# Two residual convolution layers on one core: block buffers made and first blocks loaded between the layers, a ring of three split eighths, another order of table loads, undivided stores

## The chip, the cores and the metric

The program runs on one core of one Trainium2 chip. Its metric is the device time of one execution in microseconds (us), over the whole program; less is better. TensorE (PE) multiplies matrices, VectorE (DVE) and ScalarE (ACT) work on elements, GpSimd (POOL) fills buffers and issues the stores here, and SyncE (SP) issues nearly all loads.

## The reference, cut to what matters

The input `x` is (8, 32, 512, 512) in float32. Each of two layers normalises in groups of two channels and adds its result to its input:

```python
# layer 0
x = x + quantised_conv3x3(group_norm(x))        # rounds to steps of S_X, S_OUT; clips to int8
# layer 1: g = group_norm(x)
feat = einsum('bihw,oi->bohw', g, conv_w) + conv_b        # pointwise, 32 -> 32 channels
filt = einsum('kh,bchw,lw->bckl', Ph, feat, Pw)           # 5x5 means of feat: one filter per image, channel
x = x + depthwise_conv5x5(feat, filt)                     # padded by 2
```

The statistics and the filters of layer 1 need all of layer 0's output, so the two layers can't overlap in their main work.

## The kernel before, in words

`quantised_conv` runs layer 0 and writes its result, called x1, to the output tensor in device memory. It keeps statistics (`own`) and sums over bins (`sums`) in SBUF. `statistics_of_x1` (L583) turns them into a mean and a reciprocal deviation for each image, and `filters` (L615) turns these into the filters, written to device memory as banded matrices (`table_scratch`) and bias rows (`bias_scratch`). Then `depthwise` (L757) runs layer 1 from x1 and adds its result into the output tensor. Each of the four is an `nc.Block()` of its own, with an instruction stream for each engine; a block ends on all engines before the next begins on any.

`depthwise` cuts each image into 9 blocks of 57 output rows (61 input rows), and each block into 8 steps. A step does two things:

- The pointwise product of block j. ACT makes the high half of an eighth of the block (L966, `high`), DVE the low half (L998, `low`), both float16, into a slot of the ring `c_z` (4 slots, `Z_SLOTS`). PE multiplies (L1053 to L1055, 24 matmuls), and ACT (L979) and DVE (L1024) split the product into `c_feat`, high and low.
- The banded product of block j-1 for 4 of the 32 channels: 36 matmuls of PE (L1074) with the tables `c_tt`. ACT (L988) and DVE (L1031) copy the result to `c_xr` (4 slots of one step each), and POOL adds it into the output tensor with accumulating DMAs (L925).

A group is the 8 steps of one j; there are 9 groups per image, j = 1 to 9, plus a first group with only the pointwise product of block 0. In group 9 of an image the pointwise product is already that of block 0 of the next image. A hardware loop runs over three pairs of images, and the last pair is written out.

`high` runs two steps ahead of its product (`ahead(p, e, j, s + 2)`) and `low` one step ahead. A block's input `c_x` has two slots. SP loads block j+2 into the slot of block j in step 6 of group j, by four DMAs of 976 KB (L851), after waiting until all lows of block j are done (L846).

Each image has its own tables. They come in four parts, `load_table` with g = 0 to 3 (L871, L872), and part g serves banded steps 2g and 2g+1; a part is loaded over the old one once those steps of the previous image's last block are done. SP's order in group 9 is: part 0, block j+2, part 1, part 2, part 3. In the group after it (j = 1 of the next image) banded step 0 first needs part 0, step 2 part 1, step 4 part 2, step 6 part 3 (`t_loaded`, L1064).

Ahead of layer 1, `depthwise` itself fills the constant rows and edges of `c_feat` and `c_z` (POOL L904 to L911, DVE L1033 to L1036). SP, ACT and DVE wait for this (`cleared`), and then SP loads blocks 0 and 1 and all tables.

Of the kernel before, what the change touches and what calls it, by code (L numbers as in the profile page):

```python
# [5 lines left out]
ALU = mybir.AluOpType  # L6
ACT = mybir.ActivationFunctionType
AX = mybir.AxisListType
F32 = mybir.dt.float32
# [37 lines left out]
Z_SLOTS = 4  # L47
# [535 lines left out]
def statistics_of_x1(nc, nb, k, own, mean, rstd):  # L583

    with ExitStack() as ctx:
        sem = Counted(nc, ctx)
        ps = ctx.enter_context(nc.psum_tensor("s_ps", [P, 2, 512], F32))
        gs = GroupStatistics(nc, ctx, k, sem, "s_gs", nb, ps)
        kept = sem("s_kept")
        block = ctx.enter_context(nc.Block())  # L590

        @block.sync
        def _(sp):
            sem.start(sp)

        @block.tensor
# [160 lines left out]
def depthwise(nc, nb, k, rstd, table_d, bias_d, out):  # L757
# [6 lines left out]
    with ExitStack() as ctx:  # L764
# [4 lines left out]
        xt = sb("c_x", [P, 2, ROWS_IN, P], F32)  # L769
        z = sb("c_z", [P, Z_SLOTS, 2, PAIRS_PART, P], F16)  # L770
        feat = sb("c_feat", [P, 2, 2, C, FP], F16)
# [6 lines left out]
        x1_loaded = [sem(f"c_x1_loaded{i}") for i in range(2)]  # L778
# [3 lines left out]
        stored = [ctx.enter_context(nc.semaphore(f"c_stored{i}")) for i in range(XR_SLOTS)]  # L782
        starter = sb("c_starter", [P, XR_SLOTS], F32)

        zero_rows, started, cleared = sem("c_zero_rows"), sem("c_started"), sem("c_cleared")
        zh_done, zl_done = sem("c_zh_done"), sem("c_zl_done")
        conv_done, fh_done, fl_done = sem("c_conv_done"), sem("c_fh_done"), sem("c_fl_done")
        band_done, even_out, odd_out = sem("c_band_done"), sem("c_even_out"), sem("c_odd_out")
        N = BLOCKS
# [3 lines left out]

        def valid(i):

            return (2 if i == 0 else 0), min(ROWS_IN, H + 2 - ROWS_OUT * i)
# [46 lines left out]
        def load_x1(eng, p, e, j):  # L843

            if (e, j) not in ((0, 0), (0, 1)):
                eng.wait_ge(zl_done, count(p, e, STEPS * N, STEPS * (j - 1)) + START)  # L846
            de, i = own(j)
            lo, hi = valid(i)
            r0 = ROWS_OUT * i - 2
            for q in range(Q):  # L850
                eng.dma_start(xt[C * q:C * q + C, x_slot(e, j), lo:hi, :],  # L851
                              x1v[e + de::2][p, q, :, r0 + lo:r0 + hi, :]).then_inc(x1_loaded[x_slot(e, j)], 16)
# [4 lines left out]
        def _(sp):  # L857
# [44 lines left out]
        def _(pool):  # L902
            for m in range(XR_SLOTS):
                pool.dma_start(starter[0:1, m:m + 1], rstd[0:1, 0:1]).then_inc(stored[m], 16)  # L904

            for slot in range(2):
                pool.memset(feat[96:P, slot, 0, :, :], 1.0).then_inc(started, 1)  # L907
            pool.wait_ge(started, 6 + START)
            pool.memset(feat[:, :, :, :, 0:1].rearrange("p a b c d -> p (a b c) d"), 0.0)
            pool.memset(feat[:, :, :, :, FP - 1:FP].rearrange("p a b c d -> p (a b c) d"), 0.0).then_inc(cleared, 1)  # L910
            pool.wait_ge(cleared, 1 + START)  # L911

            def group(p, e, j, pointwise, banded):
                if not banded:
                    return
                if pointwise:

                    pool.wait_ge(x1_loaded[x_slot(e, j)], loads_of(p, e, j) + START)
                for s in range(STEPS):
# [4 lines left out]
                    for lo, hi in ((0, SPLIT), (SPLIT, n)):  # L924
                        pool.dma_start(out[e::2][p, 4 * s:4 * s + 4, r0 + lo:r0 + hi, :].rearrange("c h w -> h c w"),  # L925
                                       xr_rows(m, lo, hi), accum_op=ALU.add).then_inc(stored[m % XR_SLOTS], 16)

            run(pool, group)
            for m in range(XR_SLOTS):
                pool.wait_ge(stored[m], nb * (TILES // XR_SLOTS) * 32 + 16)  # L930
# [5 lines left out]
        def split_part(t, part):  # L936
            return z[:, part % Z_SLOTS, t, :, 0:MAIN].rearrange("p j (a h) -> p j a h", a=2)

# [15 lines left out]
        def wait_slot(eng, p, e, m):  # L954
            eng.wait_ge(stored[m % XR_SLOTS], count(p, e, TILES // XR_SLOTS * 32, m // XR_SLOTS * 32) + 16)

        @block.scalar
        def _(act):
            def high(p, e, j, part):
                act.wait_ge(x1_loaded[x_slot(e, j)], loads_of(p, e, j) + START)  # L960
# [5 lines left out]
                act.activation(split_part(0, part), positions(e, j, part), ACT.Identity, scale=scale_of(e, j)).then_inc(zh_done, 1)  # L966

            def group(p, e, j, pointwise, banded):
                if not banded:
                    high(p, e, 0, 0)  # L970
                    high(p, e, 0, 1)
                elif pointwise:

                    act.wait_ge(band_done, count(p, e, TILES, STEPS * (j - 1)) + START)
                for s in range(STEPS):
                    if pointwise:
# [3 lines left out]
                        nxt = ahead(p, e, j, s + 2)  # L980
# [9 lines left out]
            act.wait_ge(cleared, 1 + START)  # L990
# [3 lines left out]
        def _(dve):  # L994
            def low(p, e, j, part):

                dve.wait_ge(zh_done, count(p, e, STEPS * N, STEPS * j + part + 1) + START)
                dve.scalar_tensor_tensor(split_part(1, part), positions(e, j, part), scale_of(e, j), split_part(0, part),  # L998
                                         ALU.mult, ALU.subtract).then_inc(zl_done, 1)

            def group(p, e, j, pointwise, banded):
                if not banded:
# [3 lines left out]
                    low(p, e, 0, 0)  # L1006
                for s in range(STEPS):
                    if pointwise and s == 3 and j == N - 2:

                        dve.wait_ge(zl_done, count(p, e, STEPS * N, STEPS * (N - 2)) + START)  # L1010
                        dve.memset(xt[:, x_slot(e, N - 1), valid(N - 1)[1]:, :], 0.0).then_inc(zero_rows, 1)
# [5 lines left out]
                    if pointwise:  # L1017
                        nxt = ahead(p, e, j, s + 1)
# [14 lines left out]
            for t in range(2):  # L1033
                dve.memset(z[:, 2 * t:2 * t + 2, :, :, MAIN:P].rearrange("p a b c d -> p (a b c) d"), 0.0).then_inc(started, 1)
            for slot in range(2):
                dve.memset(feat[96:P, slot, 1, :, :], 0.0).then_inc(started, 1)  # L1036
            dve.wait_ge(cleared, 1 + START)
# [3 lines left out]
        def _(pe):  # L1041
# [3 lines left out]
            def pointwise(p, e, j, s):  # L1045
# [4 lines left out]
                for c in range(8):  # L1050
                    zh, zl = (z[:, s % Z_SLOTS, t, c, :] for t in range(2))
# [37 lines left out]
def conv_preact_2(nc, x, w0, b0, w1, b1, out):  # L1089
# [3 lines left out]
    with ExitStack() as ctx:  # L1093
# [5 lines left out]
        k.wl = sb("w1_low", [P, Q, C], F16)  # L1099
        rstd = sb("rstd", [P, nb], F32)  # L1100
        with ExitStack() as first:
# [3 lines left out]
            k.same_group = early("same_group", [P, P], F32)  # L1105
            k.same_channel = early("same_channel", [P, P], F32)
            k.w0main = early("w0main", [P, 3, Q, C], BF16)
            k.w0edge = early("w0edge", [P, 3, C], BF16)
            k.w1t = early("w1t", [P, C], F32)
            k.wf = early("w1_diag", [P, Q, C], F32)  # L1110
            k.b0col = early("b0col", [P, 1], F32)
            k.q_bias = early("q_bias", [P, 1], F32)
            k.b1col = early("b1col", [P, 1], F32)
            k.below = early("below", [P, NBINS - 1], F32)
            k.above = early("above", [P, NBINS - 1], F32)
            k.bin_weight = early("bin_weight", [P, NBINS, NBINS], F32)
            own = early("own", [P, nb, 2], F32)
            mean = early("mean", [P, nb], F32)
            with ExitStack() as tmp:
                weights_and_masks(nc, tmp, k, w0, b0, w1, b1)  # L1120
            with nc.sbuf_tensor("sums", [P, nb, NSEG, 2 * NBINS - 1], F32) as sums:
                quantised_conv(nc, nb, k, x, out, own, sums)
                statistics_of_x1(nc, nb, k, own, mean, rstd)
                filters(nc, nb, k, sums, mean, rstd, table_d, bias_d)
        depthwise(nc, nb, k, rstd, table_d, bias_d, out)
# [26 lines left out]
```

## Time and profile before

| | |
|---|---|
| median of 3 runs | 6000.67 us (5993.56 to 6012.33) |
| profiled execution, its own time | 5992.25 us |
| its span, first to last instruction | 5990.5 us |
| PE busy | 4829.2 us (81%) |
| DVE busy | 4582.7 us (76%) |
| ACT busy | 3994.4 us (67%) |
| POOL busy | 1384.6 us (23%) |
| mean granted TensorE clock | 0.909 of full speed |

Layer 0 takes the first 2.58 ms, the work between the layers about 0.1 ms, and layer 1 the rest. An engine's time beside its own instructions is idle time; the profile says which instruction or DMA ended it. Idle time matters only on the engine that sets the end. DMA queue q1 is SP's, q0 is POOL's; a share over 100% of the 16 DMA engines means that packets overlapped.

### The profile page before, as it was taken

The page shows a single profiled execution, that of the slowest core. Times are in us where ns is not written, and L with a number is a line of the kernel's source. Part 1 is how long each engine was busy: PE and PEld are TensorE (multiplying, and loading weights), DVE is VectorE, ACT ScalarE, POOL GpSimd, SP SyncE. Part 2 cuts the span into 40 slices and gives each one's busy share as a digit, 9 for nine tenths or more (in the row PEclk, how much of TensorE's full clock was granted, in tenths as well). Part 3 has the DMA queues.
Part 4 walks back from the last instruction along what each step waited for, and adds up shares of the span by engine and source line. Part 5 has one row for each costly group of instructions (what it writes and reads, how often), then busy time and mean ns, then how long its engine had stood idle before and what let it go on. Part 6 is the DMA issues. An engine that isn't in the chain of part 4 may idle for free.

```text
span 5990.5 us, 113135 instructions
## 1 busy us (share of the span) xinstructions
PE 4829.2 (81%) x43798; PEld 3263.0 (54%) x43798; DVE 4582.7 (76%) x5363; ACT 3994.4 (67%) x2509; POOL 1384.6 (23%) x1698
## 2 busy tenths in 40 slices
PE   0767767666667767918998989989989899899899
PEld 0111111111111111207988979979979789799798
DVE  6787878777787878747887868868868778688686
ACT  1646565655555556807877868868868778688686
POOL 0111111111111111112332323323323333233233
PEclk9888878888888888958999999989999999999999
DMA  9999999999999998949999999999999999999997
GB/s 263 278 276 301 301 287 302 281 302 273 319 261 322 271 312 242 287 96 184 180 196 179 180 193 183 181 190 182 188 192 180 197 179 180 188 189 178 188 190 125
DMA packets 1065164, 1347.06 MB, mean 225 GB/s; under 512 B 78330, under 2 KB 636666, under 8 KB 1060602
## 3 DMA queue, kind: packets, MB, share of 16 engines
q1 hardware_dynamic: 749506, 657.45, 49.3%
q0 software_dynamic: 240000, 537.11, 39.9%
q10 hardware_dynamic: 75072, 144.72, 8.3%
q8 instruction: 364, 5.96, 0.4%
q14 instruction: 222, 1.82, 0.1%
HBM read 800.10 MB, written 538.84 MB: 224 GB/s over the span
## 4 chain that ended last, share of the span: by engine, by line
PE 48%; SPq 4%; DMA 2%; DVE 0%; issue 0%; POOL 0%; ACT 0%; DVEq 0%; POOLq 0%; ACTq 0%
PE c_tps L1074 36%; PE c_cps L1053 4%; PE c_cps L1054 4%; PE c_cps L1055 4%; SPq L851 3%; DMA c_tt<-bias_scratch 2%; SPq L871 1%; DMA c_x<-out_dram 1%; DVE c_z L998 0%; POOL c_feat L907 0%; ACT c_z L966 0%; DVE c_xr L1031 0%; POOL c_starter L904 0%; POOL out_dram L925 0%; ACT c_feat L979 0%
## 5 line engine op out<-in xcount | busy, mean ns | idle before, releaser
L1074 PE MATMUL c_tps<-c_feat,c_tt 123*128 123x256 f16 (+1 forms) x20736 | 2385.6, 273 | 169.3 <-DMA c_tt<-bias_scratch 167.5
L1074 PEld LDWEIGHTS c_tps<-c_feat,c_tt 123*128 123x128 f16 (+1 forms) x20736 | 1998.8, 98 | 428.1 <-DMA c_tt<-bias_scratch 134.8
L925 POOL DMA_DIRECT2D out_dram<-c_xr x1152 | 1056.5, 1054 | 2266.3 <-DVE c_xr L1031 2105.9
L440 PE MATMUL b_ps<-b_xq,w0main 128*128 128x512 bf16 x3072 | 950.1, 415 | 679.5 <-ACT b_q L398 540.3
L966 ACT ACTIVATE c_z<-c_x,c_rs 128x976 f16<-128x976 f32 x576 | 1150.2, 1997 | 116.1 <-DMA c_x<-out_dram 116.1
L1031 DVE TENSOR_SCALAR c_xr<-c_tps 57x1024 f32<-57x1024 f32 (+1 forms) x576 | 701.5, 1218 | 686.1 <-PE c_tps L1074 686.1
L998 DVE SCALAR_TENSOR_TENSOR c_z<-c_x,c_rs,c_z 128x976 f16<-128x976 f32 x576 | 1105.9, 1920 | 69.6 <-ACT c_z L966 47.0
L398 ACT ACTIVATE b_q<-b_ps,q_bias 128x1024 int8<-128x1024 f32 x512 | 547.6, 1115 | 787.3 <-DVE b_x L518 728.8
L988 ACT ACTIVATE c_xr<-c_tps 57x1024 f32<-57x1024 f32 (+1 forms) x576 | 639.2, 1110 | 629.0 <-PE c_tps L1074 628.9
L440 PEld LDWEIGHTS b_ps<-b_xq,w0main 128*128 128x128 bf16 x3072 | 225.6, 101 | 1351.3 <-issue 1094.1
L453 PE MATMUL b_ps<-b_xq,w0edge 64*32 64x512 bf16 x3048 | 918.5, 411 | 0.0
L450 PE MATMUL b_ps<-b_xq,w0edge 64*32 64x512 bf16 x3048 | 915.7, 411 | 0.0
L1053 PE MATMUL c_cps<-w_high,c_z 128*128 128x128 f16 x4608 | 813.4, 221 | 124.4 <-DVE c_z L998 112.9
L979 ACT ACTIVATE c_feat<-c_cps 122x1024 f16<-122x1024 f32 x576 | 822.7, 1428 | 121.3 <-PE c_cps L1055 119.3
L573 POOL DMA_DIRECT2D out_dram<-b_x x512 | 298.9, 584 | 2254.8 <-DVE b_cols L533 2061.7
L1024 DVE TENSOR_TENSOR c_feat<-c_cps,c_feat 122x1024 f16<-122x1024 f32 x576 | 810.2, 1407 | 7.9 <-ACT c_feat L979 7.7
L1055 PE MATMUL c_cps<-w_high,c_z 128*128 128x128 f16 x4608 | 811.7, 220 | 0.0
L1054 PE MATMUL c_cps<-w_low,c_z 128*128 128x128 f16 x4608 | 811.2, 220 | 0.0
L477 DVE BATCH_NORM_STATS2 b_stats_x<-b_stream 128x6 f32<-128x512 f32 x672 | 414.4, 680 | 438.8 <-DMA b_stream<-in_x_dram 401.9
L529 DVE BATCH_NORM_STATS2 b_stats<-b_x 128x6 f32<-128x408 f32 (+5 forms) x1520 | 645.3, 500 | 3.9
L518 DVE SCALAR_TENSOR_TENSOR b_x<-b_q,b_x 128x2048 f32<-128x2048 int8 x256 | 574.8, 2281 | 65.4 <-ACT b_q L398 65.4
L383 ACT ACTIVATE b_x<-b_x,b_shift,b_scale 128x4096 int8<-128x4096 f32 x128 | 487.0, 3805 | 139.8 <-issue 101.8
(131 smaller groups left out, 2732.2 us busy)
## 6 DMA issues: line engine op xcount, KB each, us to landing
out_dram<-b_x POOLq DMA_DIRECT2D x512, 512.0 KB, 11.2
out_dram<-c_xr POOLq DMA_DIRECT2D x576, 384.0 KB, 7.9
c_x<-out_dram SPq DMA_DIRECT2D x224, 976.0 KB, 21.9
b_stream<-in_x_dram SPq DMA_DIRECT2D x672, 256.0 KB, 12.7
b_x<-in_x_dram ACTq DMA_DIRECT2D x276, 512.0 KB, 13.3
b_x<-in_x_dram SPq DMA_DIRECT2D x276, 512.0 KB, 12.4
c_tt<-table_scratch SPq DMA_DIRECT2D x64, 576.0 KB
out_dram<-c_xr POOLq DMA_DIRECT2D x512, 72.0 KB, 9.2
```

The source lines that it names most:

```text
L440: return pe.matmul(ps[:, g % 3, j, :], k.w0main[:, d, :, :].rearrange("p r o -> p (r o)"), xq[:, n % XQ_SLOTS, 2 * i + j, d:d + W], start= ...
L450: pe.matmul(ps[0:C, g % 3, j, :], k.w0edge[P // 2:P, d, :], xq[P // 2:P, (m - 1) // JB % XQ_SLOTS, (m - 1) % JB, d:d + W], start=False, st ...
L453: pe.matmul(ps[P - C:P, g % 3, j, :], k.w0edge[0:P // 2, d, :], xq[0:P // 2, (m + 1) // JB % XQ_SLOTS, (m + 1) % JB, d:d + W], start=False ...
L925: pool.dma_start(out[e::2][p, 4 * s:4 * s + 4, r0 + lo:r0 + hi, :].rearrange("c h w -> h c w"), xr_rows(m, lo, hi), accum_op=ALU.add).then ...
L966: act.activation(split_part(0, part), positions(e, j, part), ACT.Identity, scale=scale_of(e, j)).then_inc(zh_done, 1)
L979: act.activation(dst, cps[0:MAIN, s % 2, :, :].rearrange("p j (q o) -> p o q j", q=Q), ACT.Identity).then_inc(fh_done, 1)
L998: dve.scalar_tensor_tensor(split_part(1, part), positions(e, j, part), scale_of(e, j), split_part(0, part), ALU.mult, ALU.subtract).then_i ...
L1024: dve.tensor_tensor(lo, cps[0:MAIN, s % 2, :, :].rearrange("p j (q o) -> p o q j", q=Q), hi, ALU.subtract).then_inc(fl_done, 1)
L1053: pe.matmul(dst, zh, wh, start=True, stop=False)
L1054: pe.matmul(dst, zh, wl, start=False, stop=False)
L1055: last = pe.matmul(dst, zl, wh, start=False, stop=True)
L1074: last = pe.matmul(tps[:, s % 2, o % 4, :], tt[0:rows, o, tp, 2 * d:2 * d + 2, :].rearrange("k w m -> k (w m)"), feat[0:rows, (e * N + i) ...
```

## The change

The buffers `c_x`, `c_z`, `c_feat`, the starters and their semaphores are made in a class `BlockBuffers` before `statistics_of_x1`, and the constants that the first layer shared with it now live for the whole program. Their fills and the loads of blocks 0 and 1 are issued in the statistics block. The ring `c_z` has three slots and is indexed by the running number of the eighth; `high` and `low` run one step further ahead. Table parts 0 and 1 are loaded ahead of block j+2. A step's store is one DMA of 57 rows (56 in the last block) instead of one of 48 and one of 9 (8).

```diff
-Z_SLOTS = 4
+Z_SLOTS = 3
@@ statistics_of_x1
         @block.sync
             sem.start(sp)
+            for j in range(2):
+                load_block(sp, buffers, j, x1v[0], j)
+        @block.gpsimd
+        def _(pool):
+            for m in range(XR_SLOTS):
+                pool.dma_start(buffers.starter[0:1, m:m + 1], k.b1col[0:1, 0:1]).then_inc(buffers.stored[m], 16)
+            pool.memset(feat[96:P, 0, 0, :, :], 1.0).then_inc(filled, 1)
+            pool.memset(feat[96:P, 1, 0, :, :], 1.0).then_inc(filled, 1)
+            pool.wait_ge(filled, 4 + START)
+            pool.memset(feat[:, :, :, :, 0:1].rearrange("p a b c d -> p (a b c) d"), 0.0)
+            pool.memset(feat[:, :, :, :, FP - 1:FP].rearrange("p a b c d -> p (a b c) d"), 0.0).then_inc(edged, 1)
...
         @block.vector
             gs.vector_means(dve, 0, own)
+            for slot in range(2):
+                dve.memset(feat[96:P, slot, 1, :, :], 0.0).then_inc(filled, 1)
             gs.vector_spread(dve, 0, own)
...
+            for t in range(Z_SLOTS):
+                dve.memset(z[:, t, :, :, MAIN:P].rearrange("p b c d -> p (b c) d"), 0.0)
@@
+def load_block(eng, buffers, slot, x1, i):
+    lo, hi = rows_in(i)
+    r0 = ROWS_OUT * i - 2
+    for q in range(Q):
+        eng.dma_start(buffers.xt[C * q:C * q + C, slot, lo:hi, :], x1[q, :, r0 + lo:r0 + hi, :]).then_inc(buffers.x1_loaded[slot], 16)
@@ depthwise, sync
                 if not banded:
-                    load_x1(sp, p, e, 0)
-                    load_x1(sp, p, e, 1)
                     for g in range(4):
                         load_table(p, e, g)
                 for s in range(STEPS):
-                    if pointwise and j == N and s in (5, 7):
-                        sp.wait_ge(band_done, count(p, e, TILES, TILES - STEPS + s - 3) + START)
-                        load_table(p, e + 1, (s - 5) // 2)
-                    if pointwise and j == N and s == 7:
+                    if pointwise and j == N and s in (2, 4):
+                        sp.wait_ge(band_done, count(p, e, TILES, TILES - STEPS + s) + START)
+                        load_table(p, e + 1, s // 2 - 1)
+                    if s == 6 and pointwise and (j + 2 < N or another(p, e)):
+                        load_x1(sp, p, e, j + 2)
+                    if pointwise and j == N and s == STEPS - 1:
                         for g in (2, 3):
                             sp.wait_ge(band_done, count(p, e, TILES, TILES - STEPS + 2 * g + 2) + START)
                             load_table(p, e + 1, g)
-                    if s == 6 and pointwise and (j + 2 < N or another(p, e)):
-                        load_x1(sp, p, e, j + 2)
-            sp.wait_ge(cleared, 1 + START)
@@ depthwise, gpsimd
-                    for lo, hi in ((0, SPLIT), (SPLIT, n)):
-                        pool.dma_start(out[e::2][p, 4 * s:4 * s + 4, r0 + lo:r0 + hi, :].rearrange("c h w -> h c w"),
-                                       xr_rows(m, lo, hi), accum_op=ALU.add).then_inc(stored[m % XR_SLOTS], 16)
+                    pool.dma_start(out[e::2][p, 4 * s:4 * s + 4, r0:r0 + n, :].rearrange("c h w -> h c w"),
+                                   xr_rows(m, 0, n), accum_op=ALU.add).then_inc(stored[m % XR_SLOTS], 16)
@@ depthwise, scalar
                 if not banded:
-                    high(p, e, 0, 0)
-                    high(p, e, 0, 1)
+                    for part in range(Z_SLOTS):
+                        high(p, e, 0, part)
...
-                        nxt = ahead(p, e, j, s + 2)
+                        nxt = ahead(p, e, j, s + 3)
@@ depthwise, vector
                     low(p, e, 0, 0)
+                    low(p, e, 0, 1)
...
-                        nxt = ahead(p, e, j, s + 1)
+                        nxt = ahead(p, e, j, s + 2)
@@ conv_preact_2
+        buffers = BlockBuffers(nc, ctx)
+        statistics_of_x1(nc, nb, k, own, mean, rstd, buffers, out)
+        filters(nc, nb, k, sums, mean, rstd, table_d, bias_d)
+        depthwise(nc, nb, k, rstd, buffers, table_d, bias_d, out)
```

## Rows read from the trace of the kernel before

**Rows 1.** A window of layer 1: us, busy us of PE, PEld, DVE, ACT, POOL.
```profile
2860.00:3100.00 240.00, 240.00 (x2720) 219.42 (x2718) 201.96 (x140) 199.37 (x137) 83.94 (x92) 1.00 1.02 184
```

**Rows 2.** Who waited for whom from 2830 us on: total, times, longest.
```profile
PE c_tps L1074 <- DMA c_tt<-bias_scratch: 167.5, 7, 29.1
```

**Rows 3.** Chain of waits around the first image boundary: start, us, what.
```profile
3102.17 3.95 PE c_tps L1074 x36
...
3107.46 3.96 PE c_tps L1074 x36
...
3148.34 13.50 DMA c_tt<-bias_scratch
```

**Rows 4.** Timeline of SP, then of PE, there: start, us, idle before.
```profile
3072.53 22.66 SPq L851 DMA_DIRECT2D c_x<-out_dram  x4
3095.44 8.66 SPq L871 DMA_DIRECT2D c_tt<-table_scratch  x4
3114.84 23.97 SPq L851 DMA_DIRECT2D c_x<-out_dram  x4
3139.09 9.07 SPq L871 DMA_DIRECT2D c_tt<-table_scratch  x4
...
3161.89 0.40 PE L1074 MATMUL c_tps<-c_feat,c_tt 124*128 124x256 f16 x1 [27.73 <-DMA c_tt<-bias_scratch]
```

**Rows 5.** DMA queues in windows 3030:3068, 3117:3152, 3153:3161 and 5950:5979.
```profile
q1 hardware_dynamic: 7616, 3.87, 53.0%
q0 software_dynamic: 2044, 3.33, 52.6%
...
q1 hardware_dynamic: 7979, 4.99, 74.1%
...
q1 hardware_dynamic: 188, 1.57, 103.6%
...
q0 software_dynamic: 2046, 3.28, 84.0%
```

**Rows 6.** Timelines of DVE and SP between the layers.
```profile
2586.13 0.17 DVE L227 COPY s_gs_own_mean<-own 128x8 f32<-128x8 f32 x1 [4.85 <-PEq L265]
2590.04 0.16 DVE L611 COPY mean<-s_gs_mean 128x8 f32<-128x8 f32 x1
2590.77 0.09 DVE L667 MEMSET f_blank<- 1x32 uint32 x1 [0.56 <-PEq L585]
2642.05 0.25 DVE L1034 MEMSET c_z<- 128x96 uint32 x2 [16.06 <-PEq L618]
2644.58 13.89 POOL L907 MEMSET c_feat<- 32x8256 f16 x2
2659.75 36.35 SPq L851 DMA_DIRECT2D c_x<-out_dram  x8
```

**Rows 7.** Timelines of ACT and PE at the start of layer 1.
```profile
2685.65 3.76 ACT L966 ACTIVATE c_z<-c_x,c_rs 128x976 f16<-128x976 f32 x2 [96.81 <-DMA c_x<-out_dram]
2689.54 0.29 PE L1053 MATMUL c_cps<-w_high,c_z 128*128 128x128 f16 x1 [85.87 <-DVE c_z L998]
2723.11 1.43 ACT L979 ACTIVATE c_feat<-c_cps 122x1024 f16<-122x1024 f32 x1 [0.59 <-PE c_cps L1055]
2776.53 1.93 ACT L966 ACTIVATE c_z<-c_x,c_rs 128x976 f16<-128x976 f32 x1 [19.32 <-DMA c_x<-out_dram]
2780.44 0.29 PE L1053 MATMUL c_cps<-w_high,c_z 128*128 128x128 f16 x1 [15.44 <-DVE c_z L998]
```

**Rows 8.** Window 2709:2740, DMA queue q1: packets, MB, share.
```profile
q1 hardware_dynamic: 959, 5.49, 99.3%
```

**Rows 9.** L925 issue to landing, 2860:3100 and 5970:5991; 9-row stores on the page.
```profile
DMA to landing us min/median/max: 4.8/8.5/12.7
...
DMA to landing us min/median/max: 4.7/4.9/5.4
...
out_dram<-c_xr POOLq DMA_DIRECT2D x512, 72.0 KB, 9.2
```

More of the change, by code:

```diff
@@ L580, in _, with statistics_of_x1 @@
                 pool.wait_ge(x1_stored[s], nb * 2 * LOAD + 16)
-def statistics_of_x1(nc, nb, k, own, mean, rstd):
+def statistics_of_x1(nc, nb, k, own, mean, rstd, buffers, x1):
     with ExitStack() as ctx:
@@ L589, in statistics_of_x1 @@
         kept = sem("s_kept")
+        filled, edged = sem("s_filled"), sem("s_edged")
         block = ctx.enter_context(nc.Block())
+        x1v = x1.rearrange("b c h (q w) -> b q c h w", q=Q)
+        feat, z = buffers.feat, buffers.z
         @block.sync
@@ L754, in _, with __init__, sb, rows_in @@
             sp.wait_ge(stored, 16 * (5 * lots + 1))
-def depthwise(nc, nb, k, rstd, table_d, bias_d, out):
+class BlockBuffers:
+    def __init__(self, nc, ctx):
+        def sb(name, shape, dt):
+            return ctx.enter_context(nc.sbuf_tensor(name, shape, dt))
+        self.xt = sb("c_x", [P, 2, ROWS_IN, P], F32)
+        self.z = sb("c_z", [P, Z_SLOTS, 2, PAIRS_PART, P], F16)
+        self.feat = sb("c_feat", [P, 2, 2, C, FP], F16)
+        self.starter = sb("c_starter", [P, XR_SLOTS], F32)
+        self.x1_loaded = [ctx.enter_context(nc.semaphore(f"c_x1_loaded{i}")) for i in range(2)]
+        self.stored = [ctx.enter_context(nc.semaphore(f"c_stored{i}")) for i in range(XR_SLOTS)]
+def rows_in(i):
+    return (2 if i == 0 else 0), min(ROWS_IN, H + 2 - ROWS_OUT * i)
+def load_block(eng, buffers, slot, x1, i):
[3 more added lines that the diff above has]
+        eng.dma_start(buffers.xt[C * q:C * q + C, slot, lo:hi, :], x1[q, :, r0 + lo:r0 + hi, :]).then_inc(buffers.x1_loaded[slot], 16)
+def depthwise(nc, nb, k, rstd, buffers, table_d, bias_d, out):
     with ExitStack() as ctx:
@@ L768, in depthwise @@
         sem = Counted(nc, ctx)
-        xt = sb("c_x", [P, 2, ROWS_IN, P], F32)
-        z = sb("c_z", [P, Z_SLOTS, 2, PAIRS_PART, P], F16)
-        feat = sb("c_feat", [P, 2, 2, C, FP], F16)
+        xt, z, feat = buffers.xt, buffers.z, buffers.feat
+        x1_loaded, stored = buffers.x1_loaded, buffers.stored
         tt = sb("c_tt", [P, C, 2, NSHIFT, PR], F16)
@@ L777, in depthwise @@
         tps = ctx.enter_context(nc.psum_tensor("c_tps", [P, 2, 4, HW2], F32))
-        x1_loaded = [sem(f"c_x1_loaded{i}") for i in range(2)]
         edge_loaded = sem("c_edge_loaded")
         t_loaded = [sem(f"c_t_loaded{i}") for i in range(4)]
-        stored = [ctx.enter_context(nc.semaphore(f"c_stored{i}")) for i in range(XR_SLOTS)]
-        starter = sb("c_starter", [P, XR_SLOTS], F32)
-        zero_rows, started, cleared = sem("c_zero_rows"), sem("c_started"), sem("c_cleared")
+        zero_rows = sem("c_zero_rows")
         zh_done, zl_done = sem("c_zh_done"), sem("c_zl_done")
@@ L847, in load_x1 @@
             de, i = own(j)
[L848 to L852, printed above, removed]
+            load_block(eng, buffers, x_slot(e, j), x1v[e + de::2][p, :, :, :, :], i)
         block = ctx.enter_context(nc.Block())
@@ L902, in _ @@
         def _(pool):
[L903 to L911, printed above, removed]
+            pool.wait_ge(begun, START)
             def group(p, e, j, pointwise, banded):
@@ L954, in wait_slot @@
         def wait_slot(eng, p, e, m):
-            eng.wait_ge(stored[m % XR_SLOTS], count(p, e, TILES // XR_SLOTS * 32, m // XR_SLOTS * 32) + 16)
+            eng.wait_ge(stored[m % XR_SLOTS], count(p, e, TILES // XR_SLOTS * 16, m // XR_SLOTS * 16) + 16)
         @block.scalar
@@ L965, in high @@
                     act.wait_ge(conv_done, count(p, e, TILES, STEPS * j + part - Z_SLOTS + 1) + START)
-                act.activation(split_part(0, part), positions(e, j, part), ACT.Identity, scale=scale_of(e, j)).then_inc(zh_done, 1)
+                act.activation(split_part(0, j, part), positions(e, j, part), ACT.Identity, scale=scale_of(e, j)).then_inc(zh_done, 1)
             def group(p, e, j, pointwise, banded):
                 if not banded:
-                    high(p, e, 0, 0)
-                    high(p, e, 0, 1)
+                    for part in range(Z_SLOTS):
+                        high(p, e, 0, part)
                 elif pointwise:
@@ L997, in low @@
                 dve.wait_ge(zh_done, count(p, e, STEPS * N, STEPS * j + part + 1) + START)
-                dve.scalar_tensor_tensor(split_part(1, part), positions(e, j, part), scale_of(e, j), split_part(0, part),
+                dve.scalar_tensor_tensor(split_part(1, j, part), positions(e, j, part), scale_of(e, j), split_part(0, j, part),
                                          ALU.mult, ALU.subtract).then_inc(zl_done, 1)
@@ L1010, in group @@
                         dve.wait_ge(zl_done, count(p, e, STEPS * N, STEPS * (N - 2)) + START)
-                        dve.memset(xt[:, x_slot(e, N - 1), valid(N - 1)[1]:, :], 0.0).then_inc(zero_rows, 1)
+                        dve.memset(xt[:, x_slot(e, N - 1), rows_in(N - 1)[1]:, :], 0.0).then_inc(zero_rows, 1)
                     if pointwise and s == 3 and j == N - 1 and another(p, e):
@@ L1031, in group @@
                         dve.tensor_scalar(res, conv, 1.0 / FS, None, ALU.mult).then_inc(even_out, 1)
[L1033 to L1037, printed above, removed]
+            dve.wait_ge(begun, START)
             run(dve, group)
@@ L1050, in pointwise @@
                 for c in range(8):
-                    zh, zl = (z[:, s % Z_SLOTS, t, c, :] for t in range(2))
+                    zh, zl = (z[:, (STEPS * j + s) % Z_SLOTS, t, c, :] for t in range(2))
                     dst = cps[:, s % 2, c, :]
@@ L1099, in conv_preact_2 @@
         k.wl = sb("w1_low", [P, Q, C], F16)
+        k.same_group = sb("same_group", [P, P], F32)
+        k.same_channel = sb("same_channel", [P, P], F32)
+        k.w1t = sb("w1t", [P, C], F32)
+        k.b1col = sb("b1col", [P, 1], F32)
+        k.below = sb("below", [P, NBINS - 1], F32)
+        k.above = sb("above", [P, NBINS - 1], F32)
+        k.bin_weight = sb("bin_weight", [P, NBINS, NBINS], F32)
+        own = sb("own", [P, nb, 2], F32)
+        mean = sb("mean", [P, nb], F32)
         rstd = sb("rstd", [P, nb], F32)
+        sums = sb("sums", [P, nb, NSEG, 2 * NBINS - 1], F32)
         with ExitStack() as first:
@@ L1103, in early @@
                 return first.enter_context(nc.sbuf_tensor(name, shape, dt))
-            k.same_group = early("same_group", [P, P], F32)
-            k.same_channel = early("same_channel", [P, P], F32)
             k.w0main = early("w0main", [P, 3, Q, C], BF16)
             k.w0edge = early("w0edge", [P, 3, C], BF16)
-            k.w1t = early("w1t", [P, C], F32)
-            k.wf = early("w1_diag", [P, Q, C], F32)
             k.b0col = early("b0col", [P, 1], F32)
             k.q_bias = early("q_bias", [P, 1], F32)
[L1113 to L1118, printed above, removed]
             with ExitStack() as tmp:
+                k.wf = tmp.enter_context(nc.sbuf_tensor("w1_diag", [P, Q, C], F32))
                 weights_and_masks(nc, tmp, k, w0, b0, w1, b1)
[L1121 to L1125, printed above, removed]
+            quantised_conv(nc, nb, k, x, out, own, sums)
+        buffers = BlockBuffers(nc, ctx)
+        statistics_of_x1(nc, nb, k, own, mean, rstd, buffers, out)
+        filters(nc, nb, k, sums, mean, rstd, table_d, bias_d)
+        depthwise(nc, nb, k, rstd, buffers, table_d, bias_d, out)
 _INS = ["x", "L0_conv_weight", "L0_conv_bias", "L1_conv_conv_w", "L1_conv_conv_b"]
```

16 lines of the change are left out of this document (8 added, 8 removed).

## The prediction

> **What bounds the kernel now.** I read the windows over layer 1 first. The reader is to see that PE is busy for 240 of 240 us in the steady stretch, while ACT and DVE have a sixth of it free [rows 1]. So between boundaries PE alone sets the time, and a step costs 3107.46 - 3102.17 = 5.29 us [rows 3]. Only the places where PE stands still can give anything. The list of waits names the main one: seven image boundaries, 167.5 us, all for a part of the tables [rows 2]. The second is the start of layer 1 with its 15.44 us of idle PE [rows 7], and the third the passage between the layers, from 2586 to 2689 us [rows 6, 7]. Layer 0, up to 2581 us, isn't touched.
>
> The chain at the first boundary shows why PE waits. SP issues part 0, then the four DMAs of a block from 3114.84 on, and only at 3139.09 part 1, which lands at 3148.34 + 13.50 = 3161.84 us [rows 3, 4]. PE would have wanted it 27.73 us earlier, at 3134.16. The queue rows show that this isn't SP's order alone: in 3030:3068 the loads of one block moved 3.87 MB beside 3.33 MB of stores, together 7.2 MB in 38 us, and both queues' shares add up to 106% of the 16 engines [rows 5]. A block is issued at 3072.53 and the next at 3114.84, 42.3 us apart [rows 4], and its transfer takes 38 of them. The four table parts have no gap of their own to go into.
>
> **The passage between the layers.** In the kernel before, layer 1's block begins at 2642.05 on DVE and the first matmul comes at 2689.54, 47.5 us later: memsets of 13.89 us on POOL, then the load of block 0, then 3.9 us from the first `high` (2685.65) to PE [rows 6, 7]. After the change fills and blocks are there, and what remains is a copy, a small memset (0.4 us together by their neighbours, my estimate) and the 3.9 us: 4.3 us. So 43.2 us go.
>
> Against this stands where they went. SP's eight loads took 36.35 us to issue [rows 6]. In the statistics block they start at 2586.1 and hold SP until 2622.5. DVE is done with the statistics at 2590.2, and it began the filters only after the wait at the block's end, 0.56 us later [rows 6]: every engine waits there, now for SP. The filters, the table stores and all behind them start 32.3 us later. POOL's fills (13.89 us and small ones) and DVE's lie inside SP's 36 us and cost nothing; without that cover POOL's would cost about 13 us. Net gain: 43.2 - 32.3 = 10.9 us. Both ends: if SP's issues don't hold the block's end, 43; if the loads go slower there than at 2659, down to about 5. I take 10.9, as the same DMAs on an idle queue.
>
> **The first group and its stall.** From the first `high` (2685.65) to the end of the last `c_feat` copy of group 0 (2723.11 + 1.43) it took 38.9 us [rows 7]. With three highs first (3 x 2.0) and then ACT's own 3.4 us a step (1.43 and 1.9, with a little between) it could be 6.0 + 7 x 3.4 + 1.4 = 31.2. The gain lies between 0 and 7.7; I take 4, since PE's hand-over to two PSUM slots stays.
>
> Block 2 came late in the kernel before (ACT waited 19.32 us, PE 15.44) because its load stood behind all four table parts, and these behind blocks 0 and 1 [rows 7]. Queue q1 was still full of table at 2709:2740, 5.49 MB in 31 us [rows 8]. After the change the tables have the queue to themselves from about 2642 + 32 = 2674: 6.1 MB at 5.49/31 = 177 GB/s end at about 2708. Block 2 (4.0 MB) moves 1.8 MB until the first store at some 2718, and the rest at 102 to 143 GB/s [rows 5], which is 15 to 22 us: it lands at 2733 to 2740. ACT wants it five steps into group 1, 2714 + 26 = 2740. The stall is nearly hidden: I take 14 of the 15.4, with ends at 5 and 15.4.
>
> **The boundary.** Let a step be 5.29. With `low` one step further ahead, the lows of a block are finished one step earlier, so each block load is issued one step earlier, and each block is wanted one step earlier: nothing in the steady state changes, the slack of some 3 to 4 us stays. At the boundary part 1 now goes ahead of the block, and the first part behind it is part 2, wanted two steps later. Were SP's order the cause, the stall would shrink by three steps, 15.9 us. But part 1 still passes through the same queue before part 2 lands. A part is 1488 KB (1.52 MB). Alone on the queue it takes 1.52 MB at 1.57/8 = 196 GB/s, 7.8 us; beside stores at 3.87/38 = 102 GB/s 14.9 us; at the rate of 3117:3152, 4.99/35 = 143 GB/s, 10.6 us [rows 5]. I take 11.3, since the extra part moves while stores run for two more steps. Gain per boundary 15.9 - 11.3 = 4.6 us, with ends at 1.0 and 8.1, and seven boundaries make 32 us (7 to 57). What is late next is part 2, by 27.7 - 4.6 = 23 us, then nothing: part 3 is wanted 10.6 us after it.
>
> **The ring.** Three slots with `high` three steps ahead: the slot is free once the product of step s is done, which ACT has waited for anyway to copy it. No new wait and no new instruction, so it costs nothing; ACT and DVE, busy for 83% and 84% of the steady stretch, do the same work in another order [rows 1].
>
> **The stores.** POOL saves the second issue, about 0.9 us a step, while it is idle for two thirds of the time; worth nothing except at the end, where the last of the two issues lands last: 0.5 us. 
>
> [...]
>
> **Sum.** 10.9 + 4 + 14 + 32 + 0.5 = 61 us. The profiled execution's 5992.25 (span 5990.5 and 1.75 around it) becomes 5931; it lies 8.4 us under the median of the runs, so for the median I say 6000.67 - 61 = 5940 us.
>
> **Rivals.**
> - A, slower: the 57-row store goes over three engines. 55.5/3 = 18.5 us of transfer instead of 3.5, so 4.9 - 3.5 + 18.5 = 19.9 us to landing on a quiet queue [rows 9]. A slot of `c_xr` is wanted again after 4 steps, 21.2 us, less 0.8 before issue: 20.4. Up to there it costs nothing; beyond, every step lengthens. Beside block loads landing takes 8.5 against 4.9, 1.7 times as long [rows 9], which gives up to 34 us, and (34 + 0.8)/4 = 8.7 us a step. Half way, at 27 us, a step is 6.95 us: 1.66 x 576 = 950 us more, about 6890 with the gains taken off. For it: nothing in the trace excludes it. Against it, weakly: a count of rows that 16 doesn't divide is no trouble for the 9-row store, which lands in 9.2 us [rows 9]. 17%.
> - B: SP's order is all that matters, the queue has room, and each boundary gives 15.9 us: 111 instead of 32, so 5861. For it: the issues at 3139 come right after 24 us of block issues. Against: the shares of 106%. 10%.
> - C: the queue is so full that part 1 takes its 15 us or more, and the boundaries give nothing: 29 + 0.5 us remain, 5971. The saved steps let stores run on beside the loads. 15%.
> - D, the change does not do what it says: the preload costs the passage as much as it saves and the stall of block 2 stays, with small gains at the boundary: 5975 to 6000. 6%.
> - The forecast, with its terms inside their ends: 52%, own range 5905 to 5970.
>
> **How the numbers follow.** A measurement of this kernel tells about 0.3% (18 us) from no change. Forecast, B, C and most of D are faster by more: 77%. Within 0.3% is the rest of D and the low end of C: 6%. Slower is A: 17%. The range from 5860 to 5990 takes in B, C and nearly all of D; A alone lies outside.
>
> **What would show it.** In the new profile the statistics block should last about 36 us on SP and the first matmul of layer 1 come near 2679 us (before: 2689.54); PE's wait of 15.44 should be under 3 us; the wait for tables should still occur seven times, now four steps into the group instead of two, at 17 to 25 us each; a step should stay 5.29 us. Landings of L925 near 8.5 us mean 15 engines, 16 us or more on a quiet queue mean three. The forecast fails if the boundary stalls fall below 12 us each, if they don't fall at all, or if steps lengthen.

## The result and the profile after

The changed kernel takes 6227.1 us (median of 4, 6223.02 to 6236.07) against 6000.73 us before: 1.038 times the time, interval 1.036 to 1.039. It is slower by 226 us, where 61 us less was forecast. The profiled execution spans 6221.3 us.

The waits from 2830 us on (us in total, times, longest), answering to [rows 2]:

```profile
DVE c_xr L1062 <- DMA out_dram<-c_xr: 574.0, 221, 9.0
ACT c_xr L1018 <- DMA out_dram<-c_xr: 559.2, 214, 8.7
PE c_tps L1101 <- DMA c_tt<-bias_scratch: 183.4, 7, 30.1
```

The first two rows are new: before the results are copied, DVE and ACT wait for a slot of `c_xr` whose store hasn't landed. The waits for tables are no shorter. The window 3200:3500, before and then after (columns as in [rows 1]), shows that this reaches PE in the steady stretch too, where it had never stood still (300.00 of 300 us busy, then 286.08):

```profile
3200.00:3500.00 300.00, 300.00 (x3403) 274.29 (x3401) 252.42 (x174) 249.15 (x171) 104.64 (x114) 1.00 1.01 184
```
```profile
3200.00:3500.00 300.00, 286.08 (x3174) 258.04 (x3173) 230.18 (x160) 229.17 (x158) 105.10 (x53) 0.98 0.98 168
```

The page after has the DMA totals, queue q0 (packets, MB, share) and the store's landing:

```profile
DMA packets 1547457, 1350.87 MB, mean 217 GB/s; under 512 B 560634, under 2 KB 1118970, under 8 KB 1542906
q0 software_dynamic: 722304, 541.01, 42.5%
out_dram<-c_xr POOLq DMA_DIRECT2D x512, 456.0 KB, 19.7
```

The stores move the same results, but q0 has 482,304 more packets than the 240,000 before and only 3.9 MB more (541.01 against 537.11), 8 bytes a packet. A store lands after 19.7 us, where the later of a step's two landed after 9.2 [rows 9]. The traces' packet sizes: both kernels have 131,072 packets of 2048 bytes in q0, as many as the results have rows of 512 float32 (8 x 32 x 512). Of 8 bytes there are 507,904 where there were 16,384, and of 4 bytes 17,792 where there were 27,008. So the 8-byte packets carry no results; they are called empty below.

Single stores show where they belong. In e2, whose stores are those of this kernel, q0 has no packet for 28 us before those of the store issued at 5490.48 arrive. Queue q0 in 5493:5498, before the next store's packets come, and in 5496:5498:

```profile
q0 software_dynamic: 1077, 0.16, 30.7%
```
```profile
q0 software_dynamic: 35, 0.07, 20.8%
```

The 1077 packets are 988 of 8 bytes, 13 of 4 bytes and 76 of 2048 bytes. The first two kinds have all come by 5495.62, and after that only the store's long packets come, 57 x 4 = 228 in all, and they take 20.8% of 16 engines, 3.3. Of a store of 48 rows (before, 2903.5:2905.5) and one of 56 rows (e8, 2913:2915) the same line reads:

```profile
q0 software_dynamic: 127, 0.26, 95.2%
```
```profile
q0 software_dynamic: 148, 0.30, 88.9%
```

That is 15.2 and 14.2 engines. The 48-row store has no 8-byte packet, and its 16 packets of 4 bytes come together at its end, from 2905.87 to 2906.32. The 56-row store has 32, and of its 16 packets of 4 bytes two come at 2912.8 and 14 behind the last long packet, from 2915.65 to 2915.80. So the author reads: one 4-byte packet for each engine when it is done; the 57-row store gives 76 long packets to each of three engines and 76 empty ones to each of the 13 others, 13 x 76 = 988; the 56-row store uses 14 engines and leaves 2 x 16 = 32.

The counts of the whole agree. If 9 rows go over nine engines and 8 over eight, each leaves 7 x 4 = 28 and 8 x 4 = 32 empty packets, and 512 x 28 + 64 x 32 = 16,384, the number before. The changed kernel has 512 x 988 + 64 x 32 = 507,904. One store less in each of 576 steps saves 16 packets of 4 bytes: 491,520 - 9,216 = 482,304, to the packet. The time fits too: a 2048-byte packet of q0 lasts 0.19 us on average, and 76 of them 14 us. Which engine carried a packet isn't in the trace.

The same kernel holds its own control. The last block's stores have 56 rows. L955 in 6150:6185 (57 rows, q0's stores alone) and in 6187:6221 (56 rows, at the end):

```profile
L955 POOL DMA_DIRECT2D out_dram<-c_xr x7: 2007/2009/2025, 6150.7 to 6181.3; - x7
DMA to landing us min/median/max: 16.7/17.7/18.7
...
L955 POOL DMA_DIRECT2D out_dram<-c_xr x7: 1057/1059/1075, 6191.1 to 6213.4; - x7
DMA to landing us min/median/max: 5.8/6.1/10.1
```

With no load beside either, 57 rows land after 17.7 us and 56 after 6.1; the prediction's sign for three engines was 16 us or more on a quiet queue. POOL itself needs 2.0 us to issue the one and 1.06 us for the other, which has only one row less.

The passage between the layers came as forecast, on DVE and PE (answering to [rows 6, 7]):

```profile
2587.93 0.17 DVE L227 COPY s_gs_own_mean<-own 128x8 f32<-128x8 f32 x1 [4.95 <-PEq L265]
2599.38 5.04 DVE L247 TENSOR_SCALAR s_gs_half<-s_gs_half 128x8 f32<-128x8 f32 x1
2621.97 0.09 DVE L689 MEMSET f_blank<- 1x32 uint32 x1 [16.27 <-PEq L585]
...
2678.39 0.29 PE L1080 MATMUL c_cps<-w_high,c_z 128*128 128x128 f16 x1 [43.53 <-DVE c_z L1028]
```

From the start of the statistics to the first matmul it takes 90.5 us, against 2689.54 - 2586.13 = 103.4. DVE, done with its part, waits 16.27 us for the block's end: SP issues the eight loads from 2588.36 on for 33.14 us, to 2621.50.

### The profile page after: what moved, and what is told of

It is laid out like the page before. It is cut to its first block, busy times and chain, and to the rows that moved or that the text cites. A ratio compares the mean times of both kernels' runs of the same rounds, so it can differ in the third digit from the quotient of the medians.

```text
span 6221.3 us, 111673 instructions
## 1 busy us (share of the span) xinstructions
PE 4893.7 (79%) x43798; PEld 3280.8 (53%) x43798; DVE 4574.5 (74%) x5364; ACT 3994.6 (64%) x2509; POOL 1427.7 (23%) x1122
## 2 busy tenths in 40 slices
DMA packets 1547457, 1350.87 MB, mean 217 GB/s; under 512 B 560634, under 2 KB 1118970, under 8 KB 1542906
## 3 DMA queue, kind: packets, MB, share of 16 engines
q0 software_dynamic: 722304, 541.01, 42.5%
## 4 chain that ended last, share of the span: by engine, by line
DMA 36%; SPq 10%; DVE 4%; PE 3%; issue 3%; ACT 1%; POOLq 0%; ACTq 0%; POOL 0%; DVEq 0%
DMA out_dram<-c_xr 29%; SPq L807 9%; DMA c_x<-out_dram 6%; PE c_tps L1101 3%; DVE c_xr L1062 2%; DMA c_tt<-bias_scratch 2%; SPq L913 2%; DVE c_z L1028 1%; DVE c_feat L1055 1%; ACT c_xr L1018 0%; ACT c_z L996 0%; PE c_cps L1080 0%; PE c_cps L1082 0%; PE c_cps L1081 0%; ACT c_feat L1009 0%
## 5 line engine op out<-in xcount | busy, mean ns | idle before, releaser
L1101 PE MATMUL c_tps<-c_feat,c_tt 123*128 123x256 f16 (+1 forms) x20736 | 2428.2, 276 | 375.9 <-DMA c_tt<-bias_scratch 183.4
L955 POOL DMA_DIRECT2D out_dram<-c_xr x576 | 1098.0, 1906 | 2510.8 <-DVE c_xr L1062 2077.9
## 6 DMA issues: line engine op xcount, KB each, us to landing
out_dram<-c_xr POOLq DMA_DIRECT2D x512, 456.0 KB, 19.7
c_x<-out_dram SPq DMA_DIRECT2D x224, 976.0 KB, 25.9
b_stream<-in_x_dram SPq DMA_DIRECT2D x672, 256.0 KB, 12.9
c_x<-out_dram SPq DMA_DIRECT2D x32, 944.0 KB, 25.9
```

The costliest lines, as they stand in the source:

```text
L955: pool.dma_start(out[e::2][p, 4 * s:4 * s + 4, r0:r0 + n, :].rearrange("c h w -> h c w"), xr_rows(m, 0, n), accum_op=ALU.add).then_inc(sto ...
L1101: last = pe.matmul(tps[:, s % 2, o % 4, :], tt[0:rows, o, tp, 2 * d:2 * d + 2, :].rearrange("k w m -> k (w m)"), feat[0:rows, (e * N + i) ...
```

## The experiments

In what follows, a ratio is against runs of the kernel before on the same chip, with its 95% interval. Theory T: the 57-row store on three engines makes all of the loss, and the rest of the change gains what the prediction summed. Rival R: the moved loads or the smaller ring make the loss, and the store is neutral.

**Stores divided again in the changed kernel (e1), undivided alone in the kernel before (e2).**

```diff
# e1 (e2 is the reverse, on the kernel before)
-                    pool.dma_start(... r0:r0 + n ..., xr_rows(m, 0, n), accum_op=ALU.add)
+                    for lo, hi in ((0, SPLIT), (SPLIT, n)):
+                        pool.dma_start(... r0 + lo:r0 + hi ..., xr_rows(m, lo, hi), accum_op=ALU.add)
```

> The changed kernel with its stores divided again into 48 and 9 rows, all else as changed. Theory T (the 57-row store runs on three of the 16 DMA engines and alone makes the loss): the wait of ACT and DVE for a free slot of c_xr goes (591 us on DVE after the change), the landing falls from 19.7 to about 8 us, and what is left of the change shows its own gain: 5940 us, between 5905 and 5971. Rival R (the moved loads or the three-slot ring make the loss, the store is neutral): stays near 6227.

> The kernel before with one store of 57 rows per step and nothing else. T: 6001 + (6227 - 5940) = about 6290 us, with landings near 19.7 us and 988 empty 8-byte packets per store of 57 rows. R: 6001 within 0.3%. If the store costs only together with the other order of loads, it is between.

e1: 5904.97 us, 0.985 of before (0.983 to 0.987). e2: 6323.5 us, 1.054 (1.050 to 1.058). The edit costs 1.0376 - 0.9849 = 5.3% inside the change and 5.4% alone, 316 and 324 us. R falls, and T holds for the loss: dividing the store again takes away all of it. The rest of the change is worth 91 us (79 to 103), more than the 61 that T and the forecast gave it. The signs that were on record before e2 ran came too: a landing of 19.8 us, and 722,304 packets in q0, the count that 988 empty ones a store make.

**Another division: 56 and 1 rows (e8), 51 and 6 rows (e9), both on e1.**

```diff
-                    for lo, hi in ((0, SPLIT), (SPLIT, n)):
+                    for lo, hi in ((0, 56), (56, n)) if n > 56 else ((0, 48), (48, n)):   # e8
+                    for lo, hi in ((0, 51), (51, n)):                                     # e9
```

> e1 with its stores divided into 56 and 1 rows (the last block's as in e1). Theory: a store runs on the largest number of engines up to 16 that divides its rows, so 14 and 1; the busiest engine has 16 to 20 packets of 2048 bytes, as with 48 and 9: 5905 within 0.5%. 8-byte packets: 2 x 16 + 15 x 4 = 92 per 57-row step. A theory by which a divided store is good for having two DMAs: the same.

> e1 with its stores divided into 51 and 6 rows. Engines theory: 51 = 3 x 17 goes to three engines with 68 packets each, so it is nearly as slow as the undivided store: landing near 18 us, 6150 to 6230 us in all. If it is the undivided store as such that is slow (one DMA instead of two): 5905 as e1.

e8: 5916.15 us, 0.987 (0.984 to 0.989). e9: 6554.39 us, 1.094 (1.092 to 1.096). Divided in two, the store is slow when its larger part has 51 rows (e9) and fast when it has 56 (e8). Queue q0 of e9 and of e8:

```profile
q0 software_dynamic: 756096, 541.24, 40.4%
```
```profile
q0 software_dynamic: 248192, 537.18, 40.2%
```

e9's surplus over 240,000 is 516,096, all of it packets of 8 bytes: the trace has 532,480 of them where e1 has 16,384. If 51 rows go over three engines, 6 over six and the last block's 5 over five, they leave 13 x 68 = 884, 10 x 4 = 40 and 11 x 4 = 44 empty packets, and 512 x (884 + 40) + 64 x (884 + 44) = 532,480. In e8 the time came as expected, the count didn't: 24,576 packets of 8 bytes, 8,192 more than in e1, make 28 + 16 = 44 a step in 512 steps, not 92. The 56 rows leave 32 of them, so the one-row store leaves 12, not the 60 of the expectation. Twelve is what it leaves if its four packets (one row of four channels) go over four engines. The theory of the expectation, the largest number of engines up to 16 that divides the rows, thus fits the packets of 57, 56, 51, 48, 9, 8, 6 and 5 rows and not those of one row, and it stands on these counts alone. e9 is slower than the changed kernel itself, 6554 against 6227 us, where 6150 to 6230 was expected. Its stores on the page (KB, us to landing):

```profile
out_dram<-c_xr POOLq DMA_DIRECT2D x576, 408.0 KB, 9.1
out_dram<-c_xr POOLq DMA_DIRECT2D x512, 48.0 KB, 20.3
```

This doesn't say that 51 rows land early and 6 late. Both stores of a step count on one semaphore, and each brings 16 packets of 4 bytes. As the author reads it, the profile takes the first 16 of the pair for the landing of the first store, wherever they come from: 68 packets of 0.19 us on one engine need 13 us, more than 9.1. Only the second figure tells when both have landed: 20.3 us after the second issue, which starts some 1.0 us after the first. So the slot is free 21.3 us after the first issue instead of 19.7. By estimate these 1.6 us, once in four steps, are at most 0.4 us a step and 230 us over 576 steps, of the 327 by which e9 is slower than the changed kernel. Why the pair lands later than one 57-row store, and where the rest comes from, stays open.

**Six result slots: undivided (e11) and divided (e12), on the kernel before.**

```diff
-XR_SLOTS = 4
-Z_SLOTS = 4
+XR_SLOTS = 6
+Z_SLOTS = 2
```

> The kernel before with the undivided stores (6324 us with four result slots) and six slots of c_xr; to make room the ring c_z has two slots, at the old distances, which adds no wait. If the wait for a free slot is all of the loss, a landing of 20 us is hidden behind 31.7 us of six steps: about 6000. If three engines also slow the loads of blocks and tables (waits of 152 us and 71 us more in the four-slot version), it stays well above: 6080 to 6200.

> The control of the run above: six slots, ring of two, and the divided stores (48 and 9) as before. 5993 within 0.5%: with landings of 8 us two more slots have nothing to hide, and the smaller ring adds no wait.

e12: 5994.53 us, 1.000 (0.999 to 1.002), so six slots and a ring of two change nothing by themselves. e11: 6243.88 us, 1.043 (1.040 to 1.046), somewhat above the expected band. Waits of e11 from 2830 us on; those of DVE and ACT for a slot have gone from the list:

```profile
ACT c_z L965 <- DMA c_x<-out_dram: 273.4, 42, 11.9
PE c_tps L1073 <- DMA c_tt<-bias_scratch: 219.3, 7, 33.0
```

With four slots (e2) the first was 151.8, so waits moved from the slots to the block loads. About a fifth of the loss (1.054 against 1.043) needed the slots. The rest shows in the loads: a block load lands after 25.9 us instead of 21.9. Two things about the store may do this, by the author's estimate, and no run here parts them, since they come together. One is that three engines carry a whole store, if a load needs these three as well. The other is the empty packets, which take time on the 13 others. Queue q0 in 3200:3500, before (57 steps) and after (53 stores):

```profile
q0 software_dynamic: 16463, 26.70, 53.1%
```
```profile
q0 software_dynamic: 64485, 25.08, 58.3%
```

That is 0.531 x 16 x 300 / 57 = 44.7 us of engine time for a step's stores before and 52.8 after. The 8.1 us more are near what 960 packets of 8 bytes need at 10 ns, their mean in the trace; over 16 engines they are 0.5 us a step, about what a step has grown by (316/576 = 0.55).

**The order of the tables: old order in e1 (e3), new order alone in the kernel before (e4), part 1 cut to an eighth (e10).**

```diff
# e10, on e1
-                        load_table(p, e + 1, s // 2 - 1)
+                        load_table(p, e + 1, s // 2 - 1, 8 if s == 2 else 1)   # channels of the part
```

e10 leaves work out: at each image boundary seven of part 1's eight channels keep the filters of the image before, so it shows what the bytes cost and is no kernel to use.

> The changed kernel with divided stores and the old order of table loads (part 0, block, parts 1 to 3): what is left is the preload and the ring. From the prediction's terms: e1 plus 32 us, so about 5972, if the part 1 moved ahead still has to pass through the queue (4.6 us a boundary). If SP's order alone were the cause of the boundary stall it would be 111 us slower than e1. If the order is worth nothing, it equals e1.

> The kernel before with only the new order of table loads: parts 0 and 1 ahead of block j+2. Without the earlier lows the load of the block isn't issued a step earlier, so of the three steps two are left: 10.6 - 11.3 us a boundary, about no change: 6001, between 5975 and 6010. If SP's order alone counts: 7 x 10.6 = 74 us less, 5927.

> e1 with part 1 of the next image's tables cut to an eighth of its bytes at the image boundaries (one channel instead of eight; the output of the other seven channels then uses the previous image's filters). The new table order gave nothing: is that because part 1 fills the queue ahead of part 2? If so, the table waits (115 us over seven boundaries in e1) fall by 7/8 of 11 us each, about 67 us in all, to some 50, and the time to about 5840. If the bytes don't matter, as when SP's issues or their number set the landing, both stay as in e1 (5905).

e3: 5907.78 us, 0.984 (0.981 to 0.987), not told from e1; the 32 us that the prediction's terms gave to the order didn't come. e4: 6001.04 us, 1.000 (0.998 to 1.002), as expected. e10: 5840.58 us, 0.975 (0.973 to 0.977), as expected. The table waits of e1, then of e10:

```profile
PE c_tps L1102 <- DMA c_tt<-bias_scratch: 115.1, 7, 22.1
```
```profile
PE c_tps L1102 <- DMA c_tt<-bias_scratch: 47.0, 6, 11.0
```

Seven eighths of a part fewer ahead of part 2 shorten the waits by 68 us, 9.7 a boundary, so a whole part costs about 11. Two steps gained by the order, 10.6, less 11: nothing. What PE waits for at the boundary is bytes that must pass through the queue ahead of part 2.

**The ring alone, on the kernel before (e5).**

```diff
-Z_SLOTS = 4
+Z_SLOTS = 3
-                        nxt = ahead(p, e, j, s + 2)      # high
+                        nxt = ahead(p, e, j, s + 3)
-                        nxt = ahead(p, e, j, s + 1)      # low
+                        nxt = ahead(p, e, j, s + 2)
```

> The kernel before with only the ring of three slots, high three and low two steps ahead; loads, order and stores as before. The tables were waited for 167.5 us before, 112.6 with ring and preload. If the earlier lows alone do this (each block's load issued a step earlier): 6000 - 37 to 55 us, about 5950, and the table waits near 115. If the preload does it, 6000 within 0.3% and waits near 167.

5961.3 us, 0.995 (0.994 to 0.997): 30 us less. Its table waits from 2830 us on:

```profile
PE c_tps L1075 <- DMA c_tt<-bias_scratch: 125.7, 7, 21.0
```

That is 167.5 - 125.7 = 41.8 us, 6.0 a boundary, one step and a little. The profiled execution was the fastest of e5, 20 us under its median, so the 30 us may be the truer figure, 4.3 a boundary. What takes the waits to 113 with the preload (112.6 in e3, 115.1 in e1) isn't shown; waits of the same order differ by some 9 us between executions (158.6 in e12, 167.5 before).

**Loads of blocks 0 and 1 in the filters block (e6), and the fills too (e13).**

```diff
# filters, sync (e6, on e1; taken out of statistics_of_x1)
+            for j in range(2):
+                load_block(sp, buffers, j, x1v[0], j)
             sp.wait_ge(tables_ready, 1)
# filters, gpsimd (e13, on e6): starters, edges and four fills of c_feat, two of them DVE's until then
+            pool.memset(feat[96:P, 0, 1, :, :], 0.0).then_inc(filled, 1)
+            pool.memset(feat[96:P, 1, 1, :, :], 0.0).then_inc(filled, 1)
```

> The kernel with divided stores (e1, 5905 us), but the loads of blocks 0 and 1 are issued in the filters block, while DVE computes for 35 us and SP has nothing to do, instead of in the statistics block. If SP's 33 us of issuing hold the end of the statistics block (DVE sat idle for 16 us there, after waits of its own): the statistics block shrinks to POOL's fills, about 17 us, and the table stores land a little later behind the blocks: 10 to 20 us less, about 5890. If the block's end isn't held by SP: same as e1.

> The kernel with the loads of blocks 0 and 1 in the filters block (5891 us), and now POOL's fills there too, with DVE's two fills of c_feat given to POOL. The statistics block, 22 us long with them, goes back to about 5 us, and POOL's 32 us lie beside DVE's 35: 15 to 18 us less, about 5875. If POOL's memsets slow DVE's small instructions, less; if they outlast them, nothing.

e6: 5890.71 us, 0.983 (0.981 to 0.986), the fastest kernel with the reference's work, though its interval overlaps e1's. In one execution each, the time from the statistics to the first matmul is 90.3 us in e1 and 77.6 in e6. e13: 5896.12 us, 0.983 (0.980 to 0.986), no further gain where 15 to 18 us was expected, and 85.8 us. DVE in e13, beside POOL's memsets:

```profile
2595.04 0.30 DVE L697 SCALAR_TENSOR_TENSOR f_rows<-sums,above,f_rows 128x72 f32<-128x72 f32 x1
2595.37 6.37 DVE L692 COPY f_rows<-sums 128x72 f32<-128x72 f32 x1
```

The copy takes 0.20 us elsewhere in that block, and 6.37 here, until a memset of 6.97 us ends. DVE's filters take 60 us instead of 35. The expectation named this case, and it came.

## Why the prediction was wrong

- **The stores, the step that failed.** The sum priced the undivided store at 0.5 us gained, on the condition that 57 rows are spread as 48 and 9 are. They aren't: by the packets of e2 they go over three engines, and the edit costs 5.3% to 5.4%, 316 to 324 us (e1, e2), instead of gaining 0.5. The prediction had the mechanism as rival A at 17%, with nearly the right transfer: 18.5 us over three engines and 19.9 to landing on a quiet queue, where 17.7 was measured. That 57 rows go over 15 or 16 engines in 3.5 us was the author's assumption: no run shows it, and what the runs show is three engines and 17.7 us to landing. The trace of before couldn't decide, since it has stores of 48, 9 and 8 rows only, whose counts fit 16, nine and eight engines. With no measured row behind 15 or 16, 17% for the other case was too little.
- **Its size.** A was priced at 950 us, with a landing of 27 us beside block loads; it cost 316. The landing grew only from the quiet 17.7 to a median of 19.7 over layer 1, so it lies around the 20.4 us at which a slot is wanted again, and the waits are short: 574 us over 221 times, 2.6 each. The stretch of 1.7 was read off the divided stores, which take up to 15.2 engines at a time by the share of 95.2%, and it doesn't carry over; why isn't shown. A's path to the cost was wrong in part, too: it charged everything to the slot, and by e11 that is a fifth of it.
- **The passage.** Forecast 10.9 us, measured 12.9 (103.4 to 90.5), and not by luck: the filters start 29.4 us later where 32.3 was said (34.04 - 4.64, from the statistics' start), and 42.4 us go behind that point where 43.2 was said. First matmul forecast near 2679, seen at 2678.39.
- **The first group and its stall.** Forecast 4 and 14. From the first matmul to the first result copy 38.5 us became 32.6 in e1 (5.9), and the idle time of 15.44 became 2.2.
- **The boundary.** Forecast 32 us, measured in e1 167.5 - 115.1 = 52. The reasoning on the queue was right: an extra part was forecast at 11.3 and costs about 11 by e10, and rival B (SP's order alone) falls with e3 and e4. What was too small is the worth of the earlier lows: one step, 5.3, which came to 6.0 alone (e5) and, with the order worth nothing, 7.5 with the preload (e1). With some 9 us of scatter over seven boundaries the two are hardly apart. In the changed kernel itself none of this shows: its table waits are 183.4 us, beside block loads that land after 25.9 us, where e1 has 115.1 and 21.0.
- **The ring.** No cost, as said: e12 with even fewer slots equals before. Its gain was booked under the boundary.

## What to carry to other kernels

Before merging accumulating stores like these, measure one of the merged row count: one row more or less (56, 57) made a store land after 17.7 us instead of 6.1. Here 57 = 3 x 19 and 51 = 3 x 17 rows were the slow ones, with packets that fit three engines, and 48 and 56 = 4 x 14 the fast ones, with packets that fit 16 and 14. One merged edit of this kind can bury several good ones, so time it alone. At these boundaries, with q1 at 74.1% of the 16 engines in 3117:3152 [rows 5], a new order of transfers gave nothing until bytes went. An issue loop that holds a block's end is better put where its engine has nothing else to do: it shortened the passage by 12.7 us in one execution each, though the whole time of e6 isn't clear of e1's.

## What the runs showed of the hardware

- An accumulating store from POOL, its packets per store, and the engines that they fit if each engine it doesn't use gets as many empty packets as a used one gets long ones:

| rows | of 2048 bytes | of 8 bytes | engines | seen in |
|---|---|---|---|---|
| 57 | 228 | 988 | 3 | e2, the store issued at 5490.48 |
| 56 | 224 | 32 | 14 | e8, the store issued at 2910.76 |
| 48 | 192 | 0 | 16 | before, the store issued at 2901.89 |
| 9, 8 | 36, 32 | 28, 32 | 9, 8 | before, count of the whole (16,384) |
| 51, 6, 5 | 204, 24, 20 | 884, 40, 44 | 3, 6, 5 | e9, count of the whole (532,480) |
| 1 | 4 | 12 | 4 | e8, count of the whole (24,576) |

- The page showed it: packets under 512 bytes are 78,330 before and in e1, 86,522 in e8, and 560,634 and 594,426 in the slow kernels (after and e2, e9).
- POOL's issue took 1.06 us for 56 rows (448 KB) and 2.01 us for 57 (456 KB).
- In e13 each copy of `f_rows` and `f_bins` that DVE began beside a 7 us memset of POOL took 6.3 to 6.7 us, until about the memset's end, instead of 0.20 (0.26 for `f_bins`, before), and `scalar_tensor_tensor` kept its 0.30 beside them. In the changed kernel's statistics one `tensor_scalar` (L247) took 5.04 us instead of 0.17; another (L239), which reads `s_ps`, kept its 0.17 beside the same memset.
